# Fetching the per-batch W1 matrices in two gathers of 64 in place of one of 128, and turning each half with 64-row transposes

## The reference

```python
x = x + einsum('bct,bcd->bdt', x, W0[subject])   # subject: 128 indices, 0..7
x = x + einsum('bct,bcd->bdt', x, W1[cond])      # cond: 128 indices, 1..198
return x                                          # (128, 64, 512) fp32
```

## Time and profile before

| | us |
|---|---|
| median of 3 runs | 92.8 (92.76 to 95.19) |
| the profiled execution | 92.78 |
| its span, first to last instruction | 91.0 |
| PE busy in the span | 78.5 (86%) |
| DVE, ACT, POOL busy | 61.8, 58.6, 23.4 |

### The profile page before, as it was taken

One profiled execution on the slowest core, in us unless ns is written; L12 is line 12 of the kernel. 1 busy time (PEld: TensorE's weight loads), 2 busy tenths in 40 slices (PEclk: granted clock), 3 DMA queues, 4 the chain that ended last, 5 costly groups with the idle time before them and its releaser, 6 DMA issues.

```text
span 91.0 us, 2427 instructions
## 1 busy us (share of the span) xinstructions
PE 78.5 (86%) x890; PEld 44.7 (49%) x890; DVE 61.8 (68%) x127; ACT 58.6 (64%) x117; POOL 23.4 (26%) x119
## 2 busy tenths in 40 slices
PE   0499939994999999999999999999999999999200
PEld 0389929983554544364454445445454544444000
DVE  1087008995288888796887878788777888778700
ACT  2899806886276767585777667677666777577500
POOL 3400029999999959300000000000000000000000
PEclk9999999999999999999999999999999999999995
DMA  0999989999999999999999999999999999999993
GB/s 9 334 411 421 461 342 427 412 412 407 411 411 402 412 400 414 409 421 420 418 418 414 423 420 418 416 418 421 423 407 423 418 418 421 421 414 376 414 420 140
DMA packets 9181, 35.93 MB, mean 395 GB/s; under 512 B 721, under 2 KB 850, under 8 KB 9042
## 3 DMA queue, kind: packets, MB, share of 16 engines
q1 hardware_dynamic: 4512, 16.78, 46.3%
q10 hardware_dynamic: 4514, 16.91, 45.8%
q0 software_dynamic: 144, 2.10, 5.4%
HBM read 19.01 MB, written 16.78 MB: 393 GB/s over the span
## 4 chain that ended last, share of the span: by engine, by line
PE 70%; DMA 13%; DVE 9%; issue 1%; DVEq 1%; ACTq 0%; POOLq 0%
PE psum L219 62%; DMA w_rows<-in_L_cond_weights_dram,cond 10%; DVE w L238 7%; PE psum L200 7%; DMA subjects<-in_itok_B_dram 2%; DVEq L69 1%; DVE xy L260 1%; PE psum L180 1%; DVE m_diag L252 1%; ACTq L318 0%; DVE w_rows L313 0%; POOLq L149 0%; DVEq L244 0%
## 5 line engine op out<-in xcount | busy, mean ns | idle before, releaser
L219 PE MATMUL psum<-xy,m_diag 64*128 64x512 f32 x256 | 57.1, 596 | 0.5 <-DVE m_diag L252 0.5
L260 DVE COPY xy<-psum 64x512 f32<-64x512 f32 x64 | 43.7, 683 | 13.2 <-PE psum L219 12.2
L260 ACT COPY xy<-psum 64x512 f32<-64x512 f32 x64 | 37.2, 581 | 19.8 <-PE psum L219 19.0
L219 PEld LDWEIGHTS psum<-xy,m_diag 64*128 64x128 f32 x256 | 24.8, 187 | 27.1 <-issue 25.7
L157 POOL COPY w0b<-w0t 64x64 f32 x112 | 21.6, 235 | 11.0 <-DMA w_rows<-in_L_cond_weights_dram,cond 8.5
L200 PEld LDWEIGHTS psum<-w,w0b 64*32 64x32 f32 x512 | 5.6, 105 | 6.4 <-issue 3.8
L238 ACT COPY w<-psum 64x256 f32<-64x256 f32 x16 | 5.8, 364 | 4.1 <-PE psum L180 3.1
L180 PE MATMUL psum<-ident,w_rows 128*64 128x128 f32 x64 | 7.2, 274 | 1.4 <-DVE w_rows L313 1.4
L252 DVE TENSOR_SCALAR m_diag<-psum,mask 128x256 f32<-128x256 f32 (+1 forms) x18 | 7.3, 449 | 1.1 <-PE psum L200 0.9
L326 ACT COPY w<-w_rows 128x256 f32<-128x256 f32 x18 | 7.3, 405 | 0.9 <-DMA w_rows<-in_L_cond_weights_dram 0.3
L180 PEld LDWEIGHTS psum<-ident,w_rows 128*64 128x64 f32 x64 | 7.0, 152 | 1.6 <-DVE w_rows L313 1.6
(11 more groups left out here) (8 smaller groups left out, 2.3 us busy)
## 6 DMA issues: line engine op xcount, KB each, us to landing
xy<-in_x_dram SPq DMA_DIRECT2D x15, 1024.0 KB, 19.0
out_dram<-xy ACTq DMA_DIRECT2D x15, 1024.0 KB, 11.0
xy<-in_x_dram SPq DMA_DIRECT2D x2, 512.0 KB, 5.9
out_dram<-xy ACTq DMA_DIRECT2D x2, 512.0 KB, 4.3
w_rows<-in_L_cond_weights_dram ACTq DMA_DIRECT2D x1, 128.0 KB, 2.6
cond<-in_itok_B_dram SPq DMA_DIRECT2D x1, 0.5 KB, 2.4
subjects<-in_itok_B_dram ACTq DMA_DIRECT2D x1, 0.5 KB
w_rows<-in_L_cond_weights_dram,cond POOLq DMA_INDIRECT x1, 9.5
```

What stands on the lines that cost most here:

```text
L219: last = nc.tensor.matmul(psum[:, 2 * (s % Y_RING) + h, :], m_diag[rows, odd, v % M_RING, j, :], xy[rows, s, j * T:(j + 1) * T], start=j = ...
L260: copy(xy[rows, s, i * T:(i + 1) * T], psum[HALVES[i], 2 * (s % Y_RING) + h, :]).then_inc(done, 1)
```

## The change

The gather is cut in two: gather 0 fetches the matrices of the even batches to partitions 0 to 63 of `w1_rows`, gather 1 those of the odd batches to partitions 64 to 127, each with a semaphore of its own. POOL issues one behind the other. To give each gather its indices in partitions 0 to 63, `cond` is loaded as 64 rows of 2.

Each half is turned by itself: 8 turns of 8 transposes, each transpose of 64 rows with the 64x64 corner of the identity. A turn fills one bank as before, and the copies move as many elements as before, in another pattern (8 neighbouring elements in place of 4 at the destination). VectorE adds 1 to the first half's diagonals, copies its four turns, waits for the second gather, and goes on with the second half's. The ticks are 13 in place of 18.

```diff
-    TURN = 4
+    PARTS = 2
+    PART = B // PARTS
+    TURN = BANK // PART
     TURNS = C // TURN
-    TICKS = 18
+    TICKS = 13
...
-            sp.dma_start(cond[:, :], cond_dram.rearrange("(b o) -> b o", o=1)).then_inc(s_cond, 16)
+            sp.dma_start(cond[:, :], cond_dram.rearrange("(b g) -> b g", g=PARTS)).then_inc(s_cond, 16)
...
             pool.wait_ge(s_cond, 16)
-            nc.gpsimd.indirect_dma_start(
-                out=w1_rows[:, :, :].rearrange("b d e -> b (d e)"), out_offset=None,
-                in_=w1_dram.rearrange("s d e -> s (d e)"),
-                in_offset=bass.IndirectOffsetOnAxis(ap=cond[:, 0:1], axis=0)).then_inc(s_gather, 16)
+            for g in range(PARTS):
+                part = slice(g * PART, (g + 1) * PART)
+                nc.gpsimd.indirect_dma_start(
+                    out=w1_rows[part, :, :].rearrange("b d e -> b (d e)"), out_offset=None,
+                    in_=w1_dram.rearrange("s d e -> s (d e)"),
+                    in_offset=bass.IndirectOffsetOnAxis(ap=cond[:, g:g + 1], axis=0)).then_inc(s_gather[g], 16)
...
-            pe.wait_ge(s_w1_plus, 1)
-            for n in range(TURNS):
-                if n >= W1_RING:
-
-                    before = n - W1_RING
-                    pe.wait_ge((s_w1_v, s_w1_s)[before % 2], 2 * (before // 2 + 1))
-                for z in range(TURN):
-                    last = nc.tensor.transpose(psum[0:C, n % W1_RING, z * B:(z + 1) * B],
-                                               w1_rows[:, :, n * TURN + z], ident[:, :])
-                last.then_inc(s_w1_turned, 1)
+            for g in range(PARTS):
+                part = slice(g * PART, (g + 1) * PART)
+                pe.wait_ge(s_w1_plus, g + 1)
+                for t in range(TURNS):
+                    n = g * TURNS + t
+                    if n >= W1_RING:
+
+                        before = n - W1_RING
+                        pe.wait_ge((s_w1_v, s_w1_s)[before % 2], 2 * (before // 2 + 1))
+                    for z in range(TURN):
+                        last = nc.tensor.transpose(psum[0:C, n % W1_RING, z * PART:(z + 1) * PART],
+                                                   w1_rows[part, :, t * TURN + z], ident[part, part])
+                    last.then_inc(s_w1_turned, 1)
...
+        def plus_one(g):
+            nc.vector.wait_ge(s_gather[g], 16)
+            diagonal = w1_rows[g * PART:(g + 1) * PART, :, :].rearrange("b d e -> b (d e)")[:, ::C + 1]
+            nc.vector.tensor_scalar_add(diagonal, diagonal, 1.0).then_inc(s_w1_plus, 1)
+
         def copy_w1(eng, copy, done, n):
 
             eng.wait_ge(s_w1_turned, n + 1)
-            turned = psum[0:C, n % W1_RING, :].rearrange("q (k v o r) -> q o v r k", k=TURN, o=2, r=SLOT)
+            g, t = n // TURNS, n % TURNS
+            turned = psum[0:C, n % W1_RING, :].rearrange("q (k v o r) -> q o v r k", k=TURN, o=2, r=SLOT // PARTS)
             for odd, rows in enumerate(HALVES):
-                copy(w1[rows, :, n * TURN:(n + 1) * TURN].rearrange("q (v r) k -> q v r k", r=SLOT),
+                copy(w1[rows, g::PARTS, t * TURN:(t + 1) * TURN].rearrange("q (v r) k -> q v r k", r=SLOT // PARTS),
                      turned[:, odd, :, :, :]).then_inc(done, 1)
...
-            for n in range(odd, TURNS, 2):
+            for n in range(odd, PARTS * TURNS, 2):
+                if not odd and n % TURNS == 0:
+                    plus_one(n // TURNS)
                 copy_w1(eng, copy, w1_done, n)
```

More of the change, by code:

```diff
@@ L84, in bass_cond_residual_kernel @@
         mask = sb("mask", [P, 2], fp32)
-        cond = sb("cond", [B, 1], i32)
+        cond = sb("cond", [PART, PARTS], i32)
         subjects = sb("subjects", [1, B], i32)
@@ L93, in bass_cond_residual_kernel @@
         s_w0_rows = sem("s_w0_rows")
-        s_gather = sem("s_gather")
+        s_gather = [sem(f"s_gather{g}") for g in range(PARTS)]
         s_mask = sem("s_mask")
@@ L152, in _ @@
                 if first == EARLY * UNIT:
-                    pool.wait_ge(s_gather, 16)
+                    for g in range(PARTS):
+                        pool.wait_ge(s_gather[g], 16)
                     pool.wait_ge(s_w0t, 4)
@@ L223, in apply @@
                     last.then_inc(s_y_psum, 1)
-            pe.wait_ge(s_w1_v, TURNS)
-            pe.wait_ge(s_w1_s, TURNS)
+            pe.wait_ge(s_w1_v, PARTS * TURNS)
+            pe.wait_ge(s_w1_s, PARTS * TURNS)
             products(0)
@@ L309, in _ @@
                                       w0t[HALVES[odd], bass.ds(picked[n] * C, C)]).then_inc(s_w0b_early, 1)
-            dve.wait_ge(s_gather, 16)
-            diagonal = w1_rows[:, :, :].rearrange("b d e -> b (d e)")[:, ::C + 1]
-            nc.vector.tensor_scalar_add(diagonal, diagonal, 1.0).then_inc(s_w1_plus, 1)
             copies(dve, nc.vector.tensor_copy, nc.vector.tensor_scalar_mul, s_w1_v, s_m_v, s_y_v, 0)
```

## The result

The change made the kernel slower by 8.7%: 100.35 us at best and 101.37 us in the median of 6 executions, against 92.78 us before; ratio 1.087, 95% interval 1.083 to 1.091. Some executions of either kernel take over 1.5% more than its best, whatever the change, and the ratios leave them out. I had forecast slower, with 96.8 us and at most 97.9. The profiled execution took 100.37 us, its span 98.6 us, 7.6 us more than before.

The account below looks back on a forecast made before the run. Two bounds of nearly one length, TensorE's chain and the DMA, with added DMA time costing in full: span 91.0 + 4.2 (half-rate gathers) - 0.2 (dip filled) = 95.0 us, plus 1.8 around it, 96.8 us; range 92.4 to 97.9.

Parts of the forecast that it names:

- the DMA is the second bound: Whole kernel: 35.93 MB at some 416 GB/s take 86.4 us, nearly as long as TensorE's chain.
- the dip: DMA share sinks to 0.86 from 83.0 to 84.5 us; an earlier TensorE only fills it, taken as 0.2 us.
- 64 partitions take the half rate: Gathers: half of the partitions have half of the entries, so each 1.05 MB takes 4.9 us in place of 2.45.
- The term: DMA time lost by the cut gather: 2.45 us on the first, 1.75 on the second, sum +4.2 us.
- So TensorE stays just inside it.: End of kernel: TensorE's last store lands by 94.1 us, before the DMA's own end at 95.0.
- the signs that I had named: After the change: VectorE's wait for the second gather its longest, no DMA share dip before the end, among others.
- I take 0.06: Turning of W1: each 64-row transpose takes 0.06 us, so VectorE's copies set the pace as before.
- at worst 1 us: Turning of W1: most that 64-row transposes of 0.108 us, 3.3 us more on the chain, would add to the time.
- My third rival: Slower by TensorE: full-rate gathers but 0.108 us per 64-row transpose, products 4.3 us late, 96.3 us; 3% chance.
- some 4 us without work did not lower it: TensorE's clock: it stayed at 1.00 near the end of the kernel before, despite TensorE having no work.
- 1 to 2 us: Cost to TensorE's chain if the clock fell to 1.2 GHz for a few us; at most 1 us shows.

Follow-up runs that it names:

- b_half_turns: The kernel before with only 8 of the 16 turns of W1, the rest filled with zeros: 93.03 us median, ratio 1.002.
- b_two_wide: The kernel before with its gather cut in two, each fetching 8 KB of every matrix to all 128 partitions: 93.04 us median, ratio 1.0005.
- a_ticks23: The changed kernel with 23 ticks in place of 13: 100.4 us median, ratio 1.081 to the kernel before.
- a_one_gather: The changed kernel's 64-row transposes and halves, but one gather over all 128 partitions and 18 ticks: 101.35 us median, ratio 1.080 to the kernel before.
- b_ticks_half: The kernel before, each of 18 ticks doing 6 transposes of 64 rows and columns in place of 3 of 128 by 128: 96.8 us median, ratio 1.042.
- c_pairs: The changed kernel with one gather and 18 ticks, transposes alternating between upper and lower 64 rows: 93.55 us median, ratio 1.010.

## Why the prediction was wrong

**Right: the DMA is the second bound.** An earlier TensorE wins at most what the dip holds: shown by b_half_turns, which started 3.4 us earlier and won nothing.

**Right: 64 partitions take the half rate.** 213 GB/s at a full share in place of 405 at 94.6%, both gathers in full; two gathers of 1 MB over 128 partitions kept 426. The term was +4.2 us, measured 9.6 - 4.9 = +4.7: x flowed beside the second gather (q1 has 30.5% of the engines from 14 to 17.5) but the two together moved only 181 GB/s, so nothing was given back, where I had counted 0.7. The Trainium skill ("SBUF — State Buffer", Door 1) has 64 partitions reach half of the ports; the half rate of the trace agrees with it, while which ports served, no run here shows. With this term alone the time would be 91.0 + 4.7 - 0.2 + 1.8 = 97.3 us.

**Wrong: "So TensorE stays just inside it."** This step failed. I let the products start between 22.2 and 24.7; they started at 28.43, the last copy was at 93.19, and the end went with TensorE's chain, 98.6, over 3 us behind the DMA's own 95.5 (91.0 + 4.7 - 0.2). With it failed two of the signs that I had named: VectorE never waited for the second gather, and the DMA share dipped before the end. Two terms beneath it:

- "I take 0.06" for a 64-row transpose, and the upper bound of 0.108 was "at worst 1 us". Full clock gave 0.075, so that 64 take 4.8 us against 3.6 for the copies that I took for the pace: TensorE became the bound of the turning; it does so from 0.056 on, since 8 transposes must fit into 0.45. My third rival had this mechanism, with the right sign and a 3% chance; its "about 0.09 us" is where its own numbers lose 2% of the time, not where TensorE becomes the bound. And "at worst 1 us" did not follow from the sum: TensorE's last store was to land at 94.1 against the DMA's 95.0, so 3.3 us more would have shown 2.4.
- "some 4 us without work did not lower it" may well be right (3.27 us did not in b_two_wide), but I had looked only for a gap. What took the clock down was the work itself: 64-row transposes. It stood at 1.2 GHz from 15 to 32 us, the spacing went to 0.107, and half of the main loop's first block was slow. "1 to 2 us" for a fall of the clock was too little by far, because it met the 128 transposes and not only some matmuls.

The clock weighs more than the spacing. An estimate from the trace: at 0.075 us a transpose, the second half, there at 18.9, would be turned from about 19.2 to 24.0 and the products would start at 24.9, against the 24.7 of the forecast; TensorE's chain would end its span near 94.6, still inside the DMA's 95.5, and the time would be some 97.3 us, inside the range. The fall added 3.5 us to the start and 1.0 us to the first block. No run shows this case, since the clock fell in a_ticks23 as well; so how the loss divides between the two terms stays an estimate.

The costs do not add. By the ratios, on 92.8 us: the gathers alone +6.0 us, the 64-row transposes alone +7.4, both +8.1. Each delays TensorE's start by 6 to 7 us (27.46 and 28.30 in place of 21.26), and in the changed kernel the second gather's 5 us lie under the first half's slow transposes. a_one_gather also shows that the change's loss would have stood with gathers at full rate.

## What to carry to other kernels

Read a change of a tile's height three times: for the DMA (here half of the partitions, half of the rate), for the engine that works on it (a transpose of half the size took 0.7 of the time, not half), and for the clock. Where such transposes have to stand, alternating the two halves of the rows (with the one gather of before) cost only 1% here. When two bounds are of one length, adding work to one needs the other costed as exactly, since it is no longer slack. And before hiding a load behind work, ask whether the DMA has idle time at all: here an earlier start of 3.4 us was worth nothing.

## What the runs showed of the hardware

- TensorE's clock fell, or stayed low, under unbroken work that used 64 of the 128 rows: it fell to 1.2 GHz in the changed kernel, in a_ticks23 and in a_one_gather, and did not rise in 11.7 us of 64-row ticks (b_ticks_half). When the same transposes alternated between the two halves of the rows it held through the turning (c_pairs, 0.039 us each), though it fell for 3.4 us afterwards. It held through an idle gap of 3.27 us between 128-row transposes, too (b_two_wide). Which property counts, rows or something that goes with them, these runs don't separate.
- The granted clock column reads 1.00 in the early stretches of b_ticks_half although the spacing there is that of 1.2 GHz (0.213 us from start to start against 0.109 later): at the start of a span the spacing of equal matmuls is the better witness. L165 tells the same in the kernel before, 415 ns a transpose against 274 for the same shape later.
- DMA engines that write to 64 partitions read as fully busy at half of the rate: the share was 1.01 at 213 GB/s, against 1.02 at 416 in the main loop. Share and rate have to be read together.
